# The composed filter as a two-parallel filter: three half-length products in place of four full ones

## The reference

```
x = x + S4(cond(x))          # pass 0
x = x + FFN(cond2(x))        # pass 1
cond: four modulated, demodulated convolutions of 3 taps (64 -> 64 channels):
      same, upsample by 2 + blur, same, blur + downsample by 2; biases
S4:   causal convolution along time with a kernel of 1024 taps (from the
      state matrices), plus D * u
FFN:  x W_base^T + b_base + LoRA of the 2 best of 8 experts (router softmax)
```

## Time and profile before

| | |
|---|---|
| median of 3 runs | 1510.2 us (1509.75 to 1510.54) |
| profiled execution, its own time | 1509.35 us |
| its span | 1507.6 us |
| PE busy | 1431.4 us, 95% of the span |
| DVE, ACT, POOL busy | 910.7, 472.1, 121.6 us |
| chain that ended last | PE 90% |
| mean granted TensorE clock | 0.988 of full speed |

### The profile page before, as it was taken

How to read it: one execution, slowest core, us unless ns; L and a number is a source line. 1 busy time by engine, 2 the same in 40 slices (tenths; PEclk the granted TensorE clock), 3 DMA queues, 4 the chain that set the end, 5 groups by cost and what they waited for, 6 DMA issues and landing times.

```text
span 1507.6 us, 24174 instructions
## 1 busy us (share of the span) xinstructions
PE 1431.4 (95%) x7807; PEld 1293.2 (86%) x7807; DVE 910.7 (60%) x2291; ACT 472.1 (31%) x778; POOL 121.6 (8%) x100
## 2 busy tenths in 40 slices
PE   3459999999999999999999999999999999999998
PEld 3247888888888888889899999999999999999997
DVE  5846777777777777776545455454545455554532
ACT  1024444444444444333213222222223132222210
POOL 5200000000000000002001010100101010101001
PEclk9969999999999999999999999999999999999999
DMA  4024555555555555644332424242333324242321
GB/s 154 15 57 114 156 158 165 156 155 147 158 160 155 155 152 160 143 131 102 88 98 86 112 80 118 80 113 85 95 89 97 102 85 113 80 118 80 105 67 42
DMA packets 101260, 170.59 MB, mean 113 GB/s; under 512 B 29993, under 2 KB 67378, under 8 KB 101106
## 3 DMA queue, kind: packets, MB, share of 16 engines
q1 hardware_dynamic: 100402, 168.53, 40.4%
...
...
## 4 chain that ended last, share of the span: by engine, by line
PE 90%; DVE 1%; SPq 1%; DMA 1%; ACT 0%; issue 0%; DVEq 0%; ACTq 0%
PE psum L1319 29%; PE psum L1321 28%; PE psum L1320 28%; PE psum L1360 4%; SPq L1000 1%; DMA vm_l<-vv_l 0%; SPq L1016 0%; DVE vv L1154 0%; PE psum L1453 0%; DMA x1d<-xr 0%; PE psum L247 0%; PE psum L232 0%; DVE apadf L286 0%; ACT vv_h L1066 0%; PE psum L255 0%
## 5 line engine op out<-in xcount | busy, mean ns | idle before, releaser
L1319 PE MATMUL psum<-wt_h,u_h 128*128 128x386 f32 (+1 forms) x768 | 264.2, 344 | 5.0 <-DVE de L310 2.6
L1321 PE MATMUL psum<-wt_h,u_l 128*128 128x386 f32 (+1 forms) x768 | 262.1, 341 | 0.0
L1320 PE MATMUL psum<-wt_l,u_h 128*128 128x386 f32 (+1 forms) x768 | 261.6, 341 | 0.0
L1319 PE MATMUL psum<-a_h,vm_h 128*128 128x512 f32 x512 | 209.4, 409 | 8.8 <-DMA vm_l<-vv_l 8.8
L1321 PE MATMUL psum<-a_h,vm_l 128*128 128x512 f32 x512 | 202.8, 396 | 0.0
L1320 PE MATMUL psum<-a_l,vm_h 128*128 128x512 f32 x512 | 202.3, 395 | 0.0
L1084 ACT ACTIVATE v<-psum,tabs 128x512 f32<-128x512 f32 x128 | 99.2, 775 | 255.8 <-PE psum L1321 255.7
L1319 PEld LDWEIGHTS psum<-wt_h,u_h 128*128 128x128 f32 x768 | 145.2, 189 | 7.0 <-issue 3.0
L1040 POOL TENSOR_TENSOR xo<-xr,bbase 128x1024 f32<-128x1024 f32 x32 | 86.1, 2690 | 779.9 <-DMA out_dram<-xo 710.8
L1320 PEld LDWEIGHTS psum<-wt_l,u_h 128*128 128x128 f32 x768 | 145.6, 190 | 1.3
L1321 PEld LDWEIGHTS psum<-wt_h,u_l 128*128 128x128 f32 x768 | 145.2, 189 | 0.0
...
## 6 DMA issues: line engine op xcount, KB each, us to landing
vm_h<-vv_h SPq DMA_DIRECT2D x256, 112.0 KB, 2.2
vm_l<-vv_l SPq DMA_DIRECT2D x256, 112.0 KB, 2.3
xin<-in_x_ph_dram SPq DMA_DIRECT2D x32, 512.0 KB, 3.3
xr<-in_x_row_dram SPq DMA_DIRECT2D x32, 512.0 KB, 3.2
x1d<-xr SPq DMA_DIRECT2D x64, 256.0 KB, 3.2
xin<-x1d SPq DMA_DIRECT2D x32, 512.0 KB, 3.3
xr<-x1d SPq DMA_DIRECT2D x64, 256.0 KB, 4.2
out_dram<-xo SPq DMA_DIRECT2D x32, 512.0 KB, 2.6
```

The costliest lines, as they stand in the source:

```text
L1319: nc.tensor.matmul(to, stat_h, mov_h, start=first_ and n == 0, stop=False, skip_group_check=True)
L1320: nc.tensor.matmul(to, stat_h, mov_l, start=False, stop=False, skip_group_check=True)
L1321: ins = nc.tensor.matmul(to, stat_l, mov_h, start=False, stop=end, skip_group_check=True)
```

## The change

The columns of the filter's input and output are split by parity. With taps V0..V3, even columns of the input a0, odd ones a1, the four half-length products become three: V0,V2 on one parity and V1,V3 on the other (the pair, with r = 0, 1), and the sums V0+V1, V2+V3 on the sum of both parities (the third). The even outputs are the sum of the pair; the odd ones are the third minus both.

- `composite(i, b)` becomes `pair(i, b)`: 12 matmuls of 256 columns reading `a_h`, `a_l` at a step of two, both parities in one PSUM bank (`ps_pair`); so `pair(i, 1)` waits until ScalarE has emptied the bank (`pair_out`). `third(i, b)`: 6 matmuls of 256 columns each.
- ScalarE also copies the even columns of layer 0's result (`a_f`), VectorE adds the odd ones (`as_sum`), ScalarE and GpSimd split the sum (`as_h`, `as_l`).
- The filter is copied by four DMAs in float32 (`vm_f`) after `blur`; ScalarE splits it afterwards (`vm_h`, 1024 columns), VectorE makes `vm_l`; GpSimd adds the taps in pairs (`pair_sums`, into `vm_f`), ScalarE and GpSimd split them (`vs_h`, `vs_l`).
- Outputs are combined on GpSimd in three dependent steps (`combined`), then `row_ends`.
- The split of `xin` moves: ScalarE scales `xin` in place (two operations) and copies it whole (`xs_h`), GpSimd makes `xs_l`. `s_l` moves from VectorE to GpSimd as well.
- To make room, `bt_h`, `bt_l` lie over the Toeplitz blocks: the adapters' matrix is loaded into `xo` and split at turn 33, when pass 0's last `s4` is done; the bias has no buffer of its own and is loaded into `xo` again for each tile of pass 1. Both loads leave the setup, with two ScalarE operations and one of GpSimd.

```diff
@@ SP, body(i) @@
+                if turn_is(i, TILES + 1):
+                    sp.wait_ge(s_lo, TILES)
+                    sp.dma_start(xo[:, :], d["ffn_B"]).then_inc(bt_in, 16)
...
+                if second(i - 1, c):
...
+                        sp.wait_ge(out_done, 16 * t)
+                    sp.dma_start(xo[:, :], d["b_base"].broadcast_to([P, L])).then_inc(bbase_in, 16)
...
                 if here(i + 1):
-                    sp.wait_ge(vv_hi, at(i + 1))
+                    sp.wait_ge(blur, at(i + 1, NBLUR, NBLUR - 1))
...
                     if here(i):
-                        sp.wait_ge(v_done, at(i, 2, 1))
-                    for src, dst, val, done in ((vv_h, vm_h, None, vmh_in), (vv_l, vm_l, vv_lo, vml_in)):
...
+                        sp.wait_ge(vs_lo, at(i))
+                    for b in range(2):
+                        for half_, o in ((LOW, 0), (HIGH, C)):
+                            sp.dma_start(vm_ff[half_, b, o:o + 7 * C],
+                                         vv[HALF[b], :, :].rearrange("p k c -> p (k c)")).then_inc(vm_in, 16)
                 if here(i + 3):
...
-                        sp.wait_ge(in_lo, at(i + 2, 2, 1))
+                        sp.wait_ge(in_lo, at(i + 2))
@@ GpSimd @@
+            def combined(g):
+                pool.wait_ge(pair_out, at(g, 2, 1))
+                pool.wait_ge(third_out, at(g, 2, 1))
+                G.tensor_tensor(v3[:, :, 1:H:2], v3[:, :, 1:H:2], by_odd, ALU.subtract).then_inc(v3_odd, 1)
+                pool.wait_ge(v3_odd, at(g, 2, 0))
+                G.tensor_tensor(v3[:, :, 1:H - 1:2], v3[:, :, 1:H - 1:2], v3[:, :, 2:H:2], ALU.subtract).then_inc(v3_odd, 1)
+                pool.wait_ge(v3_odd, at(g, 2, 1))
+                G.tensor_tensor(v3[:, :, 0:H:2], v3[:, :, 0:H:2], by_odd, ALU.add).then_inc(v3_val, 1)
@@ ScalarE @@
             def composed2(g):
-                act.wait_ge(blur, at(g, NBLUR, NBLUR - 1))
-                A(vv_h[:, :], vv[:, :, :].rearrange("p k c -> p (k c)"), ACT.Copy).then_inc(vv_hi, 1)
+                act.wait_ge(vm_in, 64 * (g + 1))
...
+                A(vm_h[:, :, :], vm_ff, ACT.Copy).then_inc(vm_hi, 1)
@@ TensorE @@
-                product(ps_y[:, b, :], [(vm_h[:, b, P * q:P * q + P], vm_l[:, b, P * q:P * q + P],
-                                         a_h[:, b, q:q + H], a_l[:, b, q:q + H]) for q in range(4)], True, True)\
-                    .then_inc(v_done, 1)
+                else:
+                    pe.wait_ge(pair_out, at(g, 2, 0))
+                for r in range(2):
+                    ins = product(ps_pair[:, Q * r:Q * r + Q],
+                                  [(vm_h[:, b, P * q:P * q + P], vm_l[:, b, P * q:P * q + P],
+                                    a_h[:, b, q:q + H:2], a_l[:, b, q:q + H:2]) for q in (r, r + 2)], True, True)
+                ins.then_inc(pair_done, 1)
+
+            def third(g, b):
+                if b == 0:
+                    pe.wait_ge(as_lo, at(g))
+                    pe.wait_ge(vs_lo, at(g))
+                product(ps_third[:, Q * b:Q * b + Q], [(vs_h[:, b, k, :], vs_l[:, b, k, :], as_h[:, b, k:k + Q], as_l[:, b, k:k + Q])
+                                                       for k in range(2)], True, True).then_inc(third_done, 1)
```

More of the change, by code:

```diff
@@ L26 @@
 H = L // 2
+Q = L // 4
 WCOLS = L + ER + E
@@ L1031, in body, with inputs, column_sums_low @@
+            def inputs(g):
+                pool.wait_ge(in_hi, at(g))
+                G.tensor_tensor(xs_l[:, :, 1:H + 1], xin[:, :, :], xs_h[:, :, 1:H + 1].bitcast(F32), ALU.subtract).then_inc(in_lo, 1)
+            def column_sums_low(g):
+                pool.wait_ge(as_hi, at(g))
+                G.tensor_tensor(as_l[:, :, 0:Q], a_f[:, :, :], as_h[:, :, 0:Q].bitcast(F32), ALU.subtract)\
+                    .then_inc(as_lo, 1)
             def body(i, c=None):
+                if first(i - 1, c):
+                    sum_low(i - 1)
+                if here(i):
+                    combined(i)
@@ L1157, in composed2 @@
             def composed2(g):
-                ve.wait_ge(vv_hi, at(g))
-                V.tensor_tensor(vv_l[:, :], vv[:, :, :].rearrange("p k c -> p (k c)"), vv_h[:, :].bitcast(F32), ALU.subtract)\
-                    .then_inc(vv_lo, 1)
-            def inputs(g, c):
-                c, t = place(g, c)
-                for b in range(2):
-                    ve.wait_ge(in_hi, at(g, 2, b))
-                    V.scalar_tensor_tensor(out=xs_l[:, b, 1:H + 1], in0=xin[:, b, :], scalar=tabs[:, c, T_IN, batch(t, b)],
-                                           in1=xs_h[:, b, 1:H + 1].bitcast(F32), op0=ALU.mult, op1=ALU.subtract)\
-                        .then_inc(in_lo, 1)
+                ve.wait_ge(vm_hi, at(g))
+                V.tensor_tensor(vm_l[:, :, :], vm_ff, vm_h[:, :, :].bitcast(F32), ALU.subtract)\
+                    .then_inc(vm_lo, 1)
             def layer0(g, c):
@@ L1176, in layer0 @@
                         .then_inc(a_lo, 1)
+                ve.wait_ge(odd_fix, at(g))
+                for b in range(2):
+                    ins = V.scalar_tensor_tensor(out=a_f[:, b, :], in0=ps_x[:, b, 1:H:2],
+                                                 scalar=tabs[:, c, T_S1, batch(t, b)], in1=a_f[:, b, :],
+                                                 op0=ALU.mult, op1=ALU.add)
+                ins.then_inc(as_sum, 1)
                 ve.wait_ge(a_lo, at(g, 2, 1))
```

198 lines of the change are left out of this document (127 added, 71 removed).

## The result

The changed kernel takes **1746.9 us** (median of 4 runs), the kernel before 1510.4 beside it: a ratio of 1.156, 95% interval 1.154 to 1.158. Forecast were 1583 us and at most 1655. The direction was right, the size was missed by 164 us, and neither the forecast nor any rival alone gives this time.

A forecast was written before the change was run, and what follows sets the result against it. TensorE bounded both passes before; afterwards a 20.4 us ring was to bound pass 0. From 1509.35: +98.6 for 29 pass 0 tiles, +8 for three without chunk, +8 joint, -41.9 pass 1: 1582, as median 1583 us; range 1520 to 1655.

The forecast's parts named there:

- I take 0.118, the row with the same number of columns: TensorE's pair products: 256-column matmuls at a step of two start 0.118 us apart, like adjacent ones; upper bound 0.233.
- the -1.35: TensorE per tile: matmul time falls from 5.60 to 4.25 us, shortening pass 1 from 25.9 to 24.6.
- Rival C: Pair products: reads at a step of two cost like 512 columns, 2.8 us more per tile, 1669 us; chance 0.08.
- I cost this at nothing: Pass 1: GpSimd's 12.4 us and the bias load, blocking SP some 3 us, fit within TensorE's 24.6 us tile.
- Joint, +8: Between the passes: adapters' matrix and bias loaded in series before the first output tile, +8 us, between 0 and +12.
- The ring: Pass 0: a closed chain through ScalarE, GpSimd, SP and transfers, filter landing to filter landing, 18.55 us, 20.4 with crowding.
- crowding: Pass 0's transfers: closely issued loads and stores land later, +1.8 us per tile, between 0 and 3.5.
- the first link: Pass 0: from the start of `vm_h` on ScalarE to the end of GpSimd's `xs_l`, forecast 9.2 us.
- the second 0.9 longer: Pass 0, SP's queue: from the end of `xs_l` to the second x1 store's issue, forecast 1.5 us.
- the sum at the upper end: Whole kernel with full crowding, a lap of 22.1 us in pass 0: 1639 us, before extras reaching 1655.
- `pair_out` at nothing: TensorE's second pair product: its wait for ScalarE to empty the PSUM bank costs nothing if ScalarE is not late.
- D, the clock at its low level across all of pass 0: TensorE idling lowers its clock to 1.2 GHz: 28.9 us per tile in pass 0, about 1857 us; chance 0.03.

The follow-up runs named there:

- removing the link: The changed kernel with ScalarE and GpSimd handling the next input before the filter and the column and pair sums: 1865.7 us, 1.234.
- The last run: Against the kernel one run earlier (1522.4 us), router's Exp moved forward, GpSimd's later sums behind the router's result, ends' scaling behind residual and router: 1470.5 us, 0.9735.
- three of the kernels above: The changed kernel with adjacent columns (1666.9 us); with reordering, planes and moved small operations (1620.5 us); the latter with filter and chunk splits reordered (1611.2 us).

## Why the prediction was wrong, step by step

- **The step that failed first: "I take 0.118, the row with the same number of columns".** It measured 0.228, the other end of my bounds. Choosing by the number of columns was wrong; the size was 24 x 0.11 = 2.65 us a tile. In pass 1 the -1.35 became +1.35, 31 x 2.65 = 82 of the 164 us missed. Rival C had the mechanism and I gave it 0.08. In pass 0 it cost nothing, as C said.
- **The step that failed second: "Pass 1. (...) I cost this at nothing", with GpSimd's 12.4 us "to hide in".** GpSimd did fit, but VectorE stood still beside it, and the router behind that: 1.76 us a tile (29.03 - 27.26, with GpSimd's operations cut short), 31 x 1.76 = 55 us. Moving the small operations alone gave back 1.28 of it. I treated two engines that hold each other up as independent.
- **Joint, +8.** The loads cost less than I took (4.5 in the laps, 2.9 in all). But laps 28 to 37 grew by 62.7; four laps of pass 0 at 3.5 and six of pass 1 at 3.1 make 32.6 of it, the loads 4.5, and 26 are left, which no term had. The 17.1 us of one wait, for the router behind a filter that is split only after landing, are the largest piece. In these laps TensorE's waits sum to 43 us (4.5 before): 23.0 for the router, 8.3 for the residual, 8.8 for VectorE's and GpSimd's parts of the ends; and the granted clock is 0.80 from 800 to 850. No run took these apart. With the two steps above this makes 82 + 55 + 22 (the 26, less the 3.5 by which the loads stayed under 8) = 159 of the 164 us.
- **The ring: right in its links, and not the whole truth.** 20.5 against 20.4, but in part by luck: crowding 1.6 against 1.8 with its two halves the wrong way round, the first link 0.4 shorter, the second 0.9 longer. (The window from which I took the filter's DMA work, 4.6, also holds the issues of `xin` and the chunk; and the sum at the upper end is 1637, not 1639.) And removing the link did not shorten the lap: 20.6, with VectorE, held three times, in its place. A number that comes out is no proof that its mechanism is the only one.
- **`pair_out` at nothing: right in the changed kernel**, where the waits of PE name other causes, and wrong once ring, small stalls and the residual's queue were gone (2.5 us a lap).
- **TensorE, -1.35: right for adjacent columns.** The last run shows it whole, 25.92 to 24.65 in pass 1. Its 16.64 in pass 0 is 1.0 above 15.65; TensorE waits there 7.6 us from 300 to 500, twelve times, for `c_l` and the pads.
- **D, the clock at its low level across all of pass 0:** it did not come. The changed kernel's granted clock is 0.97 in the windows from 200 to 500 and 1.00 in pass 1; three of the kernels above had 0.91, 0.88 and 0.93 in pass 0, where TensorE was busy 85 to 89% of the time.
